# Two fused VectorE operations in place of a ScalarE and two GpSimd steps in a graph normalisation

## The reference, cut to what matters

```
def layer(h, params):                       # runs twice per graph
    a = softmax(h @ h.T / sqrt(D))
    delta = a * adjacency
    attn = delta / (sum(delta, -1) + 1e-10)
    ctx = (attn*upper) @ hl + diag(attn) * hs + (attn*lower) @ hr
    o = (ctx - mean(ctx)) / sqrt(var(ctx) + 1e-12) * g + beta
    return relu(o)

x = layernorm(x + layer(layer(x)))
x = layernorm(x + attention(x, adj))        # 12 heads
```

## Time and profile before

| | |
|---|---|
| time, median of 3 runs | 2427.14 us (2426.58 to 2428.47) |
| span of the profiled execution | 2426.4 us |
| TensorE (PE) busy | 2020.7 us, 83% |
| DVE busy | 1771.7 us, 73% |
| ACT busy | 1289.2 us, 53% |
| POOL busy | 751.3 us, 31% |
| share of the chain that ended last: PE, DVE, ACT, POOL | 59%, 21%, 7%, 0% |

### The profile page before, as it was taken

The page is one execution under the profiler, slowest core; times in us unless marked ns, Lnnn a source line. Parts: engine busy times, 40 slices in busy tenths (PEclk is TensorE's granted clock), DMA queues, the critical chain, the costliest instruction groups (busy, mean ns, idle before and its releaser), DMA issues.

```text
span 2426.4 us, 50154 instructions
## 1 busy us (share of the span) xinstructions
PE 2020.7 (83%) x14656; PEld 1882.5 (78%) x14656; DVE 1771.7 (73%) x5318; ACT 1289.2 (53%) x3612; POOL 751.3 (31%) x778
## 2 busy tenths in 40 slices
PE   4788888888888888888888888888888888888884
PEld 4788778788877788778788777788877788778773
DVE  4577777787777777777777777777777777777764
ACT  2355555555555555455555555555455555455553
POOL 0232333332333332333332333332333332333331
PEclk8999999999999999999999999999999999999975
DMA  2222222112222112222112222112222112222111
GB/s 91 63 55 73 65 67 54 48 51 71 65 67 54 48 52 71 65 67 54 49 50 71 65 67 54 48 52 71 65 67 54 47 52 71 65 67 54 42 49 45
DMA packets 144358, 144.77 MB, mean 60 GB/s; under 512 B 17596, under 2 KB 144328, under 8 KB 144328
## 3 DMA queue, kind: packets, MB, share of 16 engines
q1 hardware_dynamic: 133424, 131.20, 20.1%
q10 hardware_dynamic: 10904, 13.20, 1.6%
HBM read 56.25 MB, written 12.58 MB: 28 GB/s over the span
## 4 chain that ended last, share of the span: by engine, by line
PE 59%; DVE 21%; issue 11%; ACT 7%; DVEq 1%; ACTq 0%; SPq 0%; POOL 0%; DMA 0%; POOLq 0%
PE bank_w L360 27%; PE bank_m L360 9%; PE bank_u L360 6%; PE bank_p L501 6%; PE bank_s L360 3%; DVE pT_lo L858 3%; PE bank_o L360 3%; DVE masked L852 3%; ACT pT_hi L654 3%; DVE normed L808 2%; PE bank_t L377 1%; PE bank_u L440 1%; PE bank_t L388 1%; ACT hlrh L596 1%; DVE tmp_a L778 1%
## 5 line engine op out<-in xcount | busy, mean ns | idle before, releaser
L647 ACT ACTIVATE prob<-masked,hmin 128x256 f32<-128x256 f32 x768 | 383.5, 502 | 154.9 <-DVE hmin L852 153.0
L852 DVE CUSTOM_DVE_ANT_0 masked<-bank_s,bias_adj 128x256 f32<-128x256 f32 x768 | 291.8, 417 | 53.9 <-PE bank_s L360 45.1
L858 DVE TENSOR_TENSOR pT_lo<-bank_p,pT_hi 128x512 f16<-128x512 f32 x384 | 262.6, 684 | 93.2 <-ACT pT_hi L654 93.2
L654 ACT ACTIVATE pT_hi<-bank_p 128x512 f16<-128x512 f32 x384 | 228.3, 594 | 155.5 <-PE bank_p L501 147.9
L501 PE MATMUL bank_p<-ident,prob 128*128 128x128 f32 x1536 | 245.9, 284 | 77.4 <-DVE pT_lo L858 69.9
L754 DVE TENSOR_TENSOR hlrl<-bank_w,hlrh 128x384 fp32r<-128x384 f32 x256 | 139.3, 554 | 203.4 <-ACT hlrh L596 203.4
L596 ACT ACTIVATE hlrh<-bank_w 128x384 fp32r<-128x384 f32 x256 | 124.0, 485 | 291.3 <-PE bank_w L360 291.2
L501 PEld LDWEIGHTS bank_p<-ident,prob 128*128 128x128 f32 x1536 | 183.7, 145 | 101.7 <-issue 60.3
L986 POOL TENSOR_TENSOR normed<-normed,g_row 128x384 f32<-128x384 f32 x64 | 63.3, 1011 | 559.4 <-ACT normed L616 559.4
L360 PE MATMUL bank_w<-hT_ach,w_qkvh 128*128 128x256 f32 x576 | 198.4, 345 | 18.5 <-DVE qk_lo L830 12.5
L360 PE MATMUL bank_w<-w_graph0h,hT_ach 128*128 128x384 f32 x576 | 204.1, 354 | 10.5 <-DVEq L711 9.9
(11 more groups left out here) (200 smaller groups left out, 6236.1 us busy)
## 6 DMA issues: line engine op xcount, KB each, us to landing
x_in<-in_x SPq DMA_DIRECT2D x64, 384.0 KB, 3.3
adj_in<-in_adj SPq DMA_DIRECT2D x96, 256.0 KB, 2.8
q_st<-qk_hi SPq DMA_DIRECT2D x256, 96.0 KB, 2.2
k_st<-qk_hi SPq DMA_DIRECT2D x256, 96.0 KB, 2.2
q_st<-qk_lo SPq DMA_DIRECT2D x128, 96.0 KB, 2.2
k_st<-qk_lo SPq DMA_DIRECT2D x128, 96.0 KB, 2.2
out<-result ACTq DMA_DIRECT2D x32, 384.0 KB, 2.5
prob<-in_L_gnn_Wl SPq DMA_DIRECT2D x2, 192.0 KB, 3.6
```

What stands on the lines that cost most here:

```text
L647: nc.scalar.activation(prob[:, h % 2, i, :], masked[:, i, :], ACT.Exp, bias=hmin[:, i, h:h + 1], scale=-1.0, accum_out=hsum[:, i, h:h + 1] ...
L654: nc.scalar.activation(pT_hi[:, h % 2, :, :].rearrange("p j i -> p (j i)"), bank_p[:, :], ACT.Copy).then_inc(s_pt_hi, 1)
L852: ve.tensor_tensor_reduce(masked[:, i, :], bank_s[:, i * S:(i + 1) * S], bias_adj[:, i, :], -SCALE, BIG, ALU.add, ALU.min, hmin[:, i, h:h ...
L858: ve.tensor_tensor(pT_lo[:, h % 2, :, :].rearrange("p j i -> p (j i)"), bank_p[:, :], pT_hi[:, h % 2, :, :].rearrange("p j i -> p (j i)"), ...
```

## The change

On DVE, `b_apply` no longer makes `shift`. After `refine` it issues four full-size operations: for each of the two tiles (mixed - mean) * g2_row, then for each tile (that * rstd) + b2_row. The ACT step, the POOL step and the tile `shift` are taken out, and with them the semaphores `s_shift` and `s_affine_mid`. `s_scaled` and `s_affine` are now both raised by DVE. The place of `b_apply.0` in DVE's order stays as it was.

```diff
@@ ORDER
-        a_proj.0 b_norm.0 a_proj.1 weights.3 scores.5 b_apply.0 a_turn.0 weights.4 ...      (act)
+        a_proj.0 b_norm.0 a_proj.1 weights.3 scores.5 a_turn.0 weights.4 ...
-        q.0 c_sum.0 q.2 v.0 b_turn.0 v.1 b_apply.0 a_turn.0                                 (pool)
+        q.0 c_sum.0 q.2 v.0 b_turn.0 v.1 a_turn.0
@@ ScalarE
-            def b_apply(t, _k):
-                act.wait_ge(s_shift, t)
-                for i in range(NT):
-                    nc.scalar.activation(normed[:, i, :], mixed[:, i, :], ACT.Identity, bias=shift[:, i:i + 1],
-                                         scale=rstd["b"][:, i:i + 1]).then_inc(s_scaled, 1)
@@ VectorE
             def b_apply(t, _k):
                 refine("b", t - 1, inv_s["b"][:, :])
-                ve.scalar_tensor_tensor(shift[:, :], mv["b"][:, :, 0], -1.0, rstd["b"][:, :], ALU.mult, ALU.mult
-                                        ).then_inc(s_shift, 1)
+                for i in range(NT):
+                    ve.scalar_tensor_tensor(normed[:, i, :], mixed[:, i, :], mv["b"][:, i, 0:1], g2_row[:, :],
+                                            ALU.subtract, ALU.mult).then_inc(s_scaled, 1)
+                for i in range(NT):
+                    dve.wait_ge(s_scaled, NT * (t - 1) + i + 1)
+                    ve.scalar_tensor_tensor(normed[:, i, :], normed[:, i, :], rstd["b"][:, i:i + 1], b2_row[:, :],
+                                            ALU.mult, ALU.add).then_inc(s_affine, 1)
@@ GpSimd
-            def b_apply(t, _k):
-                s = t - 1
-                for i in range(NT):
-                    pool.wait_ge(s_scaled, NT * s + i + 1)
-                    gp.tensor_tensor(normed[:, i, :], normed[:, i, :], g2_row[:, :], ALU.mult).then_inc(s_affine_mid, 1)
-                for i in range(NT):
-                    pool.wait_ge(s_affine_mid, NT * s + i + 1)
-                    gp.tensor_tensor(normed[:, i, :], normed[:, i, :], b2_row[:, :], ALU.add).then_inc(s_affine, 1)
```

More of the change, by code:

```diff
@@ L56 @@
         c_store.0 turn_x.2 weights.0 b_proj.5 scores.1 scores.2 a_scores.0 weights.1 scores.3 weights.2 scores.4
-        a_proj.0 b_norm.0 a_proj.1 weights.3 scores.5 b_apply.0 a_turn.0 weights.4 scores.6 weights.5 scores.7
+        a_proj.0 b_norm.0 a_proj.1 weights.3 scores.5 a_turn.0 weights.4 scores.6 weights.5 scores.7
         a_proj.2 weights.6 scores.8 a_proj.3 weights.7 a_proj.4 b_norm2.0 scores.9 a_proj.5 weights.8 turn_y.0
@@ L69 @@
     "pool": """
-        q.0 c_sum.0 q.2 v.0 b_turn.0 v.1 b_apply.0 a_turn.0""",
+        q.0 c_sum.0 q.2 v.0 b_turn.0 v.1 a_turn.0""",
 }
@@ L183, in graph_attention_kernel @@
         eps = {"a": EPS_GRAPH, "b": EPS_GRAPH, "y": EPS_NORM, "c": EPS_NORM}
-        shift = sb("shift", [P, NT])
         inv_s2 = {k: sb(f"inv_s2_{k}", [P, NT]) for k in "ab"}
@@ L228, in graph_attention_kernel @@
         s_self, s_diag = sem("s_self"), sem("s_diag")
-        s_shift, s_scaled, s_affine, s_affine_mid = sem("s_shift"), sem("s_scaled"), sem("s_affine"), sem("s_affine_mid")
+        s_scaled, s_affine = sem("s_scaled"), sem("s_affine")
         s_hinv, s_csum, s_csum_mid = sem("s_hinv"), sem("s_csum"), sem("s_csum_mid")
@@ L661, in _ @@
                 "h_norm": lambda t, k: root("a", t - 1), "b_norm": lambda t, k: root("b", t - 1),
-                "b_norm2": lambda t, k: root("y", t - 1), "b_apply": b_apply, "c_norm": c_norm, "c_store": c_store,
+                "b_norm2": lambda t, k: root("y", t - 1), "c_norm": c_norm, "c_store": c_store,
                 "q": lambda t, k: qk(t, 0, k), "k": lambda t, k: qk(t, 1, k), "v": v, "scores": scores, "weights": weights, "late_weights": lambda t, k: weights(t - 1, k),
@@ L1014, in _ @@
                 "a_turn": lambda t, k: graph_turn(layer_a(t)), "b_turn": lambda t, k: graph_turn(layer_b(t)),
-                "q": q, "v": v, "b_apply": b_apply, "c_sum": c_sum,
+                "q": q, "v": v, "c_sum": c_sum,
                 "split": lambda t, n: pool.wait_ge(s_setup, n + 1),
```

## The result

The changed kernel takes 2500.5 us (median of 4 runs, 2498.4 to 2501.4) against 2427.8 us before: 2.97% slower, a ratio of 1.0297 (95% interval 1.0283 to 1.0312). The forecast was 2485 us in a range of 2464 to 2506. The sign, the place and the range hold; the rise is 72.7 us where 57 had been forecast.

What follows compares the result with a forecast made beforehand. The prediction took DVE, which PE waits for at `scores.6`, to bound the kernel; 2427.1 + 48.7 (31 graphs x 1.57 us) + 9 for the clock gave 2485 us, range 2464 to 2506.

Steps and rivals of the forecast that it cites:

- The bound: Around `b_apply`, PE's `scores.6` waits for DVE's `scores.5`; PE, 0.2 to 0.3 us early, has no slack.
- What the four operations cost: Four DVE operations in `b_apply` at 0.48 us, 1.92 us; net 1.57 us per graph, at most 1.97.
- What `shift` gives back: On DVE, the small `shift` and its issue hole leave: 0.35 us from start to start.
- The removed ACT and POOL work at nothing: ACT loses 1.29 us and POOL 3.96 us per graph; nobody waits for either, so worth nothing.
- Not given back later: PE's 0.69 us before `weights.6` and DVE's 0.53 before `weights.4` shift too; lower end 1.04 per graph.
- The clock: Longer graphs shift the low-clock stretches, leaning to the long kind: 0.3 us per graph, 9 us, ends -19 and +22.
- The sum: Whole kernel: 2427.1 + 48.7 + 9 = 2484.8, said as 2485 us, 2.4% slower.
- Absorption: DVE's idle time soon after takes up the whole delay: 2427 us, no change; chance 0.03.
- a gain: Removing ACT's 1.29 us block ahead of the `weights.4` copies brings PE forward: -0.25 us per graph, 2419; chance 0.03.
- rival 3: Clock falls at the hole before `scores.6`: 1.30 us in each graph, 40 us, 2516; chance of most graphs 0.07.
- Rival 4: New operations take longer than L808 by contention or pointer scalars: 0.69 us each, 75 us, 2502; chance 0.06.

Runs made afterwards that it cites:

- The half addition: One fused operation per tile (mixed * rstd + b2_row) in place of two, in the changed kernel: 2472.4 us, ratio 1.0179.
- the kernel with ACT and POOL loaded: Changed kernel with two activations on ACT and four products and sums on POOL put back, into y_in, beside the fused operations: 2503.9 us, ratio 1.0310.
- the kernel before with q.2 late: Kernel before with POOL's 1.80 us sum q.2 moved behind v.1 instead of ahead of v.0: 2390.9 us, ratio 0.9845.

## Why the prediction was right, and where it was off

- **The bound.** That DVE is what PE waits for at `scores.6`, and that PE has nothing to give there, is right: the hole is 1.89 us and the step from head 4 to 5 grew by 1.78. The hole was 0.12 us in every graph before, so PE came 0.12 us early and not 0.2 to 0.3 as read from the starts of its matmuls; nothing hangs on that. The half addition gives the slope: two operations 0.72, four 1.78.
- **What the four operations cost.** The prediction took 4 x 0.48 from L808. They take 0.53 each, because their scalar is read through a pointer where L808 has an immediate; the run with immediates has 0.47 (1.88 us for four). This term was 0.2 us per graph too small, 1.57 for 1.78, or 6.5 us in all. The measured value lies inside its ends, 1.57 and 1.97. The first-layer step L794 with two pointers at 0.48 was the wrong row to reassure with: it is another operation.
- **What `shift` gives back.** The 0.35 us were credited to shift and its issue hole. The sum was right, the reason half wrong: with `shift` taken out and nothing put in, the masking comes no sooner. The 0.35 us are not `shift`'s work but a hole that other work of DVE can fill; what makes the hole, the runs don't show.
- **The removed ACT and POOL work at nothing.** Right for ACT and for the load as such (the kernel with ACT and POOL loaded). Wrong in one consequence: the prediction said that POOL's `a_turn` starts a little earlier and that this helps nobody. It hurts: the products now stand in another phase to `b_resid.0`, whose record went from 0.69 to 0.98 us, 0.29 us per graph or 9 us. The row with the 0.69 was read, and "b_resid is as before" was written all the same. It was also read as contention with the product at 1105.17, which starts later than the residual step (1104.94): the step had waited for the product ahead of that one, and the product at 1105.17, with its 1.05, waited for the step. This is the term that was missing.
- **Not given back later.** Right: none of PE's later holes took up anything.
- **The clock.** 0.3 us per graph was forecast, and 0.20 is left for it, so the size was near. The description was too weak, though. The mixture of three kinds of graph did not shift, it froze into a single kind of 75.09 us; and around that point the rest moves against the work, so that neither 0.25 us less nor 0.33 us more on DVE changes the time by more than 1.1 us. In the order of DVE's work the column "rest" has +0.51, +0.46, +0.20, -0.13, then +0.78. The kernels with immediates and with POOL's products later, 1.82 and 1.80 us of added work in different places, have 0.46 and 0.48. So the rest seems to follow the length of the work, and the mean of the lengths seen before was no measure of it. That it is the clock's is argued from where the low stretches stand and from the time at 1.2 GHz; no run holds the clock fixed.
- **The sum.** 1.78 + 0.29 + 0.20 = 2.27 us per graph, 31 of them 70.4 us, and the rise of the span is 70.1 us. The forecast's 57.7 had 1.57 + 0.3: two terms too small by 0.21 and 0.29, one too large by 0.1. That the error was no larger owes something to luck as well, since nearly the same total, 2498 to 2504 us, came out of all five kernels with 1.8 to 2.4 us of added work. One slip in the working: its own range took nothing off for the clock at the lower end; 2427 + 32 - 19 is 2440, not 2459. The stated range doesn't rest on it.
- **The rivals.** Absorption and a gain didn't come. A new low stretch (rival 3) didn't come in this kernel, but it is close: 0.63 us more of DVE's time brings it in some graphs, and so does another distance between graphs. Rival 4's contention didn't touch the new operations, since POOL is idle there, but the next one down the line; its pointer scalars did come, at 0.05 us each in place of 0.21.

Open is what ties the low stretches to a fixed distance such that 75.09 or 75.10 us comes out in five kernels (and 71.65 us in the kernel before with q.2 late, where nearly all graphs of the loop are alike too). The traces show that it does, not by which rule. Open too is why, behind the same hole, a low stretch comes in some graphs and not in others.

## What to carry to other kernels

Before you move work onto an engine with idle time, look at who waits for it at that very place: 74% busy DVE had no free microsecond between two heads. When an operation is priced from a similar row, match the kind of its scalar operands and its neighbours on the other port too, and check what the removed work had kept from colliding. And when a kernel's graphs or tiles come in several lengths with the granted clock changing among them, price a change from the steps between fixed instructions, not from the total: here a relief of 8 us showed as nothing, and a kernel with less work than before was slower. Such a mean has to be taken over whole turns of the lengths.

## What the runs showed that I had not expected

- The same DVE operation (SCALAR_TENSOR_TENSOR on 128x384 fp32) takes 0.62 us with a pointer scalar and 0.56 with an immediate.
- At this place ahead of the masking small operations of DVE are nearly free: `shift` cost nothing, and of 0.35 us more 0.07 was visible.
- A loop whose work changes from 5.23 to 5.81 us in one step keeps its mean period at 75.09 to 75.10 us; a further 0.30 us costs 1.21.
- A POOL sum of 1.80 us beside `h_apply` cost 37 us of 2428 in the kernel before. With q.2 early or late, three of the small refine operations just ahead of the L794 take 0.81 to 0.94 us beside other work of POOL, where those of `b_apply` take 0.15 to 0.16; whether that is the same contention, no run tests.
